# Spreading a pooled row and a bias over the partitions by transfers through device memory in a fused gate-and-attention kernel

## The reference

```
x  = x + gate(gn(x)) * gn(x)                # gn: group norm, 32 groups of 4 channels
x  = x + attention(gn(x))

gate:      pooled[c] = mean over the pixels
           pos[k, c] = clip(c + k - 1 + conv3(pooled)[k, c], 0, 127)      # 3 taps
           out[c]    = sum_k w[k] * (linear interpolation of pooled at pos[k, c]) + b
           gate[c]   = sigmoid(out[c])
attention: value = Wv x + bv;  key, query = two layers of 1x1 conv + batch norm + relu
           27 neighbours (3 x 3 at distances 1, 2 and 4), softmax of query . key over them
           context = sum of weight * value;  out = Wo context + bo
```

## Time and profile before

| | |
|---|---|
| median of 3 runs | 1546.72 us (1544.78 to 1551.17) |
| profiled execution | 1545.68 us, of which span 1543.9 us |
| TensorE busy | 1481.4 us (96%), clock 0.997 of full speed |
| VectorE, ScalarE, GpSimd busy | 1211.6, 1168.4, 776.1 us |
| chain that ended last | TensorE 78%, ScalarE 7%, VectorE 5%, transfers 3% |
| x load, store of 1568 KB, issue to landing | 7.2 us, 5.4 us (medians of 32) |

### The profile page before, as it was taken

The page is one execution under the profiler, slowest core; times in us unless marked ns, Lnnn a source line. Parts: engine busy times, 40 slices in busy tenths (PEclk is TensorE's granted clock), DMA queues, the critical chain, the costliest instruction groups (busy, mean ns, idle before and its releaser), DMA issues.

```text
span 1543.9 us, 35552 instructions
## 1 busy us (share of the span) xinstructions
PE 1481.4 (96%) x9287; PEld 1199.6 (78%) x9287; DVE 1211.6 (78%) x4620; ACT 1168.4 (76%) x3044; POOL 776.1 (50%) x2194
## 2 busy tenths in 40 slices
PE   1899999999999999999999999999999999999998
PEld 1587878888887888878888888888887887878776
DVE  6587878888887887878888888888878887878766
ACT  2577777777777777777777777777777777777776
POOL 5544455555465454455454455545455544455520
PEclk9999999999999999999999999999999999999999
DMA  3135453435453445553445553435454445453324
GB/s 132 47 106 160 151 160 114 136 112 162 149 163 107 137 114 154 156 157 113 136 116 155 156 162 113 139 107 162 149 163 119 135 114 154 148 163 113 96 67 138
DMA packets 104276, 205.98 MB, mean 133 GB/s; under 512 B 13584, under 2 KB 83600, under 8 KB 95888
## 3 DMA queue, kind: packets, MB, share of 16 engines
q1 hardware_dynamic: 104080, 203.72, 44.3%
HBM read 51.62 MB, written 51.38 MB: 67 GB/s over the span
## 4 chain that ended last, share of the span: by engine, by line
PE 78%; ACT 7%; DVE 5%; issue 5%; DMA 3%; SPq 1%; POOL 1%; ACTq 0%; DVEq 0%; POOLq 0%
PE ps_s L416 18%; PE ps_o L449 15%; PE ps_p L471 11%; PE ps_v L489 10%; PE ps_p L466 9%; PE ps_t L428 9%; DMA ksp<-kk 3%; PE ps_o L454 3%; ACT eT L599 2%; ACT e L584 2%; DVE e L946 1%; ACT qq L610 1%; ACT hid L634 1%; DVE e L929 1%; SPq L359 1%
## 5 line engine op out<-in xcount | busy, mean ns | idle before, releaser
L584 ACT ACTIVATE e<-e,zmin 128x256 f32<-128x256 f32 x800 | 404.1, 505 | 209.8 <-DVE zmin L929 201.8
L929 DVE CUSTOM_DVE_ANT_0 e<-ps_s,mask 128x256 f32<-128x256 f32 x800 | 337.3, 422 | 150.2 <-PE ps_s L416 144.1
L449 PEld LDWEIGHTS ps_o<-eT,v 128*128 128x128 f32 x2688 | 377.8, 191 | 74.0 <-issue 69.6
L449 PE MATMUL ps_o<-eT,v 128*128 128x128 f32 x2688 | 433.8, 276 | 0.5 <-ACT eT L599 0.3
L416 PE MATMUL ps_s<-kk,qq 128*128 128x256 f32 x1408 | 428.0, 386 | 0.0
L428 PE MATMUL ps_t<-ident,e 128*128 128x128 f32 x1600 | 306.0, 273 | 0.2 <-DVE e L946 0.2
L428 PEld LDWEIGHTS ps_t<-ident,e 128*128 128x128 f32 x1600 | 225.4, 141 | 81.1 <-DVE e L946 0.5
L599 ACT ACTIVATE eT<-ps_t 128x512 f32<-128x512 f32 (+1 forms) x416 | 235.0, 565 | 63.8 <-PE ps_t L428 61.6
L946 DVE SCALAR_TENSOR_TENSOR e<-e,rz,keep 128x256 f32<-128x256 f32 x480 | 251.6, 524 | 0.0
L416 PEld LDWEIGHTS ps_s<-kk,qq 128*128 128x128 f32 x1408 | 221.4, 192 | 35.7 <-issue 29.5
L471 PE MATMUL ps_p<-hid,w2T 128*128 128x448 f32 x448 | 214.6, 561 | 9.7 <-ACT hid L634 9.7
(11 more groups left out here) (147 smaller groups left out, 1917.8 us busy)
## 6 DMA issues: line engine op xcount, KB each, us to landing
raw<-in_x_dram SPq DMA_DIRECT2D x32, 1568.0 KB, 7.2
out_dram<-raw SPq DMA_DIRECT2D x32, 1568.0 KB, 5.4
v<-v SPq DMA_DIRECT2D x192, 224.0 KB, 3.2
kk<-kk SPq DMA_DIRECT2D x192, 112.0 KB, 2.2
ksp<-kk SPq DMA_DIRECT2D x192, 64.0 KB, 2.5
v<-v_last SPq DMA_DIRECT2D x64, 128.0 KB, 2.9
kk<-kk SPq DMA_DIRECT2D x32, 224.0 KB, 2.9
v<-v_last SPq DMA_DIRECT2D x64, 96.0 KB, 2.7
```

Source lines behind the costliest of these rows:

```text
L449: last = nc.tensor.matmul(o[:, UPIX * (u - 1):UPIX * (u + 1)], v[:, s, u, :], eT[:, UPIX * (base + 2 * u - 1):UPIX * (base + 2 * u + 1)], ...
L584: nc.scalar.activation(e[:, i, :], e[:, i, :], ACT.Exp, bias=zmin[:, i:i + 1], scale=-1.0, accum_out=zs[:, i:i + 1]).then_inc(e_done.next( ...
L929: nc.vector.tensor_tensor_reduce(e[:, i, :], ps_s[(TILES * n.parity() + t) % 2][:, 0:KEYS], mask[:].rearrange("p s h a b -> p (s h a b)"), ...
```

## The change

The row `pooled_row` and the row `bias` no longer come from products. The pooled column `PL` (128 partitions, one float each) is written by a transfer (s1) to a 4 x 128 scratch in device memory, `spread_row`, and read back into all partitions by a second one (s2). `c6` multiplies by the column `Y_B` instead of by `yb_row`, which gives one column; VectorE adds the constant part into the column `VB`, and two more transfers (s3, s4) spread it as `bias`. `diag`, `yb_row`, `bv_row`, the product c3 and VectorE's copy of its result are gone; `wobv` becomes a column. All four transfers are issued by SyncE, at the head of its slot, and each waits for the one before. The slots:

| step | before | after |
|---|---|---|
| LOAD | 15 | 13 |
| s1, s2, s3, s4 | - | 18, 19, 35, 36 |
| c3 | 19 | gone (19 kept for the tables) |
| d4 / a4, p4 | 20 / 21 | 22 / 23 |
| d6, a6 / d7, p7 | 25 / 26 | 26 / 27 |
| c4 / d9, p9 | 27 / 28 | 28 / 29 |
| c6 / d13 | 36 / 37 | 33 / 34 |

```diff
-LOAD = 15
+LOAD = 13
+CH = dict(aggr=12, c1=13, d1=14, c2=15, d3=16, p3=16, s1=18, s2=19, c3=19, d4=22, a4=23, p4=23, d6=26,
+          a6=26, d7=27, p7=27, c4=28, d9=29, p9=29, c5=30, d11=31, p11=31, pw=32, c6=33, d13=34, s3=35, s4=36)
+CHAIN_READS = ((2, "d1"), (4, "d3"), (13, "d9"), (15, "d11"), (17, "d13"))
...
# SyncE, called at the head of its slot
+                    def chain(m, at):
+                        i = m.parity()
+                        if at == CH["s1"]:
+                            sp.wait_ge(pg.sem, pg.count(m, 6))
+                            sp.wait_ge(pooled_in.sem, pooled_in.count(m + -2, 16))
+                            sp.dma_start(spread_row[i, :].unsqueeze(1), col(PL)).then_inc(pooled_out.next(16), 16)
+                        if at == CH["s2"]:
+                            sp.wait_ge(pooled_out.sem, pooled_out.count(m, 16))
+                            sp.wait_ge(dg.sem, dg.count(m + -1, 10))
+                            sp.dma_start(pooled_row[:], spread_row[i, :].partition_broadcast(P)
+                                         ).then_inc(pooled_in.next(16), 16)
+                        if at == CH["s3"]:
+                            sp.wait_ge(dg.sem, dg.count(m, 17))
+                            sp.wait_ge(bias_in.sem, bias_in.count(m + -2, 16))
+                            sp.dma_start(spread_row[2 + i, :].unsqueeze(1), col(VB)).then_inc(bias_out.next(16), 16)
+                        if at == CH["s4"]:
+                            sp.wait_ge(bias_out.sem, bias_out.count(m, 16))
+                            sp.wait_ge(v_done.sem, v_done.count(m + -2, COLUMNS))
+                            sp.dma_start(bias[:, i, :], spread_row[2 + i, :].partition_broadcast(P)
+                                         ).then_inc(bias_in.next(16), 16)
...
# TensorE
-                        if at == CH["c3"]:
-                            pe.wait_ge(pg.sem, pg.count(m, 7))
-                            nc.tensor.matmul(ps_v[:, 8:8 + P], ones[:], diag[:], start=True, stop=True).then_inc(cg.next(), 1)
...
-                            nc.tensor.matmul(ps_v[:, P:2 * P], yb_row[:], wvoT[:], start=True,
+                            nc.tensor.matmul(ps_v[:, 1:2], wvoT[:], col(Y_B + m.parity()), start=True,
...
# GpSimd
-                                  lambda: gp.tensor_scalar(diag[:], ident[:], col(PL), None, ALU.mult))
...
-                                  lambda: gp.tensor_scalar(yb_row[:], ones[:], col(Y_B + i), None, ALU.mult),
...
# VectorE
+                            dve.wait_ge(bias_in.sem, bias_in.count(m, 16))          # values, b == 0
...
-                            dve.wait_ge(cg.sem, cg.count(m, 3))
-                            step(5, nc.vector.tensor_copy(pooled_row[:], ps_v[:, 8:8 + P]))
+                            dve.wait_ge(pooled_in.sem, pooled_in.count(m, 16))      # d4
...
-                            step(18, nc.vector.tensor_tensor(bias[:, m.parity(), :], ps_v[:, P:2 * P], wobv[:],
-                                                             ALU.add))
+                            dve.wait_ge(bias_out.sem, bias_out.count(m + -1, 16))
+                            step(17, nc.vector.tensor_tensor(col(VB), ps_v[:, 1:2], wobv[:], ALU.add))
```

More of the change, by code:

```diff
@@ L394, in _ @@
                         slot(n, t)
-                    for transfers in x_in + stored + k_copied + [v_copied]:
+                    for transfers in x_in + stored + k_copied + [v_copied, pooled_out, pooled_in, bias_out, bias_in]:
                         sp.wait_ge(transfers.sem, transfers.here)
@@ L772, in chain @@
                         if at == CH["p9"]:
-                            gp.wait_ge(dg.sem, dg.count(m, 14))
-                            steps(23,
+                            gp.wait_ge(dg.sem, dg.count(m, 13))
+                            steps(22,
                                   lambda: gp.tensor_tensor(col(BM), col(D1), col(M1), ALU.subtract),
@@ L900, in tables @@
                             nc.vector.tensor_scalar(w2_s[:], w2_s[:], bn_s[:, 1:2], None, ALU.mult).then_inc(v_w, 1)
-                            nc.vector.tensor_scalar(bv_row[:], ones[:], bv_s[:, 0:1], None, ALU.mult).then_inc(v_w, 1)
+                            dve.wait_ge(v_w, 2)
                         if t == CH["d3"] + 1:
@@ L1002, in chain @@
                                                                accum_out=col(POS + k)).then_inc(dg.next(), 1)
-                            dve.wait_ge(dg.sem, dg.count(m, 8))
-                            step(9, nc.vector.tensor_tensor(col(POS, 3), col(POS, 3), base_f[:], ALU.add))
-                            step(10, nc.vector.tensor_scalar(col(POS, 3), col(POS, 3), 0.0, P - 1.0, ALU.max, ALU.min))
+                            dve.wait_ge(dg.sem, dg.count(m, 7))
+                            step(8, nc.vector.tensor_tensor(col(POS, 3), col(POS, 3), base_f[:], ALU.add))
+                            step(9, nc.vector.tensor_scalar(col(POS, 3), col(POS, 3), 0.0, P - 1.0, ALU.max, ALU.min))
                         if at == CH["d6"]:
-                            dve.wait_ge(pg.sem, pg.count(m, 15))
-                            step(11, nc.vector.scalar_tensor_tensor(junk[:], pooled_row[:], 1.0, hat_sum[:],
+                            dve.wait_ge(pg.sem, pg.count(m, 14))
+                            step(10, nc.vector.scalar_tensor_tensor(junk[:], pooled_row[:], 1.0, hat_sum[:],
                                                                    ALU.mult, ALU.mult, accum_out=col(ZS)))
@@ L1011, in chain @@
                             dve.wait_ge(ag.sem, ag.count(m, 4))
-                            step(12, nc.vector.tensor_scalar(col(EX), col(EX), 1.0, None, ALU.add))
-                            step(13, nc.vector.reciprocal(col(GATE), col(EX)))
+                            step(11, nc.vector.tensor_scalar(col(EX), col(EX), 1.0, None, ALU.add))
+                            step(12, nc.vector.reciprocal(col(GATE), col(EX)))
                         if at == CH["d9"]:
-                            dve.wait_ge(cg.sem, cg.count(m, 4))
@@ L1019, in chain @@
+                            step(14, nc.vector.scalar_tensor_tensor(col(SQ1), col(D1), col(D1), col(AV),
                                                                     ALU.mult, ALU.add))
                         if at == CH["d11"]:
+                            dve.wait_ge(cg.sem, cg.count(m, 4))
+                            step(15, nc.vector.tensor_scalar(col(VE1), ps_v[:, 3:4], EPS, None, ALU.add))
+                        if at == CH["d13"]:
                             dve.wait_ge(cg.sem, cg.count(m, 5))
-                            step(16, nc.vector.tensor_scalar(col(VE1), ps_v[:, 3:4], EPS, None, ALU.add))
```

76 lines of the change are left out of this document (38 added, 38 removed).

## The result

The changed kernel takes 2034.66 us (median of 4 runs, 2027.51 to 2036.74) against 1547.33 us before (median of 4 runs too): 1.314 times as long, 95% interval 1.310 to 1.318. The forecast was 1723 us. The sign and both places of loss were right, the size was not: 487 us were lost where 176 were forecast.

What follows compares the result with a forecast made beforehand. TensorE was taken as the bound, busy 1481.4 of 1543.9 us. 1545.7 - 6.6 (products) + 105 (gate) + 70 (load) + 8 (start) = 1722, as median 1723 us; own range 1677 to 1785, wider range 1610 to 1790.

Steps and rivals of the forecast that it cites:

- both places of loss: TensorE waiting for M1 before c4, +3.5 us an image, and for keys 6 in slot 17, 2.4 us.
- TensorE's products: Slot 19 loses the spread of `diag`, 0.22 us an image, 6.6 us less; narrowing c6's second product wins 0.
- The gate's slots: Later hats make VectorE wait 1.7 us at d6 and delay c4: +3.5 us an image, 105 us (75 to 135).
- The load in front of the keys: With LOAD = 13 keys 6 land behind the load; TensorE waits 2.4 us in slot 17, 29 images, 70 us.
- the 1.9 us of the forecast without s4's delay: Slot 17's wait for keys if small writes take 1.6 us and s4 costs SyncE nothing; 29 x 1.9 = 55 us.
- The four small transfers: s1 to s4 at 2.5 us each; pooled row hidden, s4 holding SyncE 0.5 us before value copies, load, keys 6.
- keep 1.6 and 4.7: Bounds for a small transfer: a 5 KB load at 1.6 us, the 0.5 KB load of `bv_s` at 4.7 us.
- the upper bounds of all parts: Gate's slots 135 us, slot 17's wait for keys 133 us (29 x 4.6), start 14 us.
- The start: Before the first scores nothing hides image 0's chain: +4.5 us, image 1's gate 3.5; together +8 us (2 to 14).
- Rival 4: Small writes slow: s3 at 4.7 us or more makes SyncE the second bound; 1785 us or more, chance 0.09.

Runs made afterwards that it cites:

- b2_load13: The kernel before with LOAD = 13 instead of 15 alone, so the load stands in front of keys 6; 1689.28 us (1.089).
- x6_grouped: The changed kernel with only the scratch laid out in groups of 8 words, 512 bytes from group to group; 1877.56 us (1.212).
- x5_apart: The changed kernel with the words of s1 and s3 written 2 KB apart, s2 and s4 reading a row of x instead; 1851.01 us (1.194).
- b4_d6: The kernel before, products kept, with c3 21, d4 22, a4 and p4 23, d6 and a6 28, later gate steps moved along; 1601.88 us (1.034).
- v1_pooled: The kernel before with the pooled row by transfers in groups of 8 words, bias still by product, LOAD = 15, later gate slots; 1528.98 us (0.987).
- x7_all: The changed kernel with scratch in groups of 8 words, LOAD = 15 and later slots, both rows by transfers; 1543.95 us (0.998).

## Why the prediction was wrong, point by point

**TensorE's products: right.** Slot 19 is 1.63 us instead of 1.85, the 0.22 us of the sum. The narrowed product of c6 wins nothing, as the prediction had it from the earlier trace rows: in the kernel after, slots 8, 9 and 11 together are as long as before (2.22 + 1.93 + 2.07 = 6.22 us, before 1.85 + 1.87 + 2.52 = 6.24), although c6 moved from one to the other.

**The gate's slots: place, chain and waits right, size short by the clock.** GpSimd's p4 and VectorE's d6 after, on their timelines:

```profile
1005.81 0.30 POOL L773 TENSOR_SCALAR hats<-hats 128x128 f32<-128x128 f32 x1 [25.39 <-ACT hats L667]
...
1010.15 0.45 POOL L777 TENSOR_TENSOR hat_sum<-hat_sum,hats 128x128 f32<-128x128 f32 x1
...
1013.95 0.27 POOL L790 TENSOR_TENSOR g<-g,st 128x1 f32<-128x1 f32 x1
```

```profile
1010.64 0.29 DVE L1029 SCALAR_TENSOR_TENSOR junk<-pooled_row,hat_sum 128x128 f32<-128x128 f32 x1 [1.68 <-POOL hat_sum L777]
```

p4 runs from 1005.81 to 1010.60, 4.8 us as in the earlier trace rows. VectorE waited 1.68 us for it (forecast 1.7), and c4 2.49 us for M1 (forecast 761.9 to 764.2, 2.3). Slots 0 to 3 are 3.2 us longer than before (forecast 3.3). Slot 4 at the start of the image (950.55 to 955.03) is 1.7 us longer, where the forecast had 0.2. In all +5.0 us against +3.5.

**The load in front of the keys: right in kind.** b2_load13 has no s4, so its wait is to be set beside the 1.9 us of the forecast without s4's delay: slot 16 is 2.9 us longer in the image shown and 3.1 in the median one. The keys landed 9.1 us after the load's issue, where 8.2 were forecast. "Lands behind it" is not to be taken to the letter: there the kk copy, issued 0.7 us after the load, took 7.4 us and landed at 956.94, 0.2 us before the load, and the second ksp copy 0.8 us after it. What the sum lacked besides is the 1.7 us of slots 17 and 18 behind it.

**The four small transfers: the step that failed.** "I take 2.5 us ..., and keep 1.6 and 4.7." It took 6.9 us, outside both bounds. The nearest row by name, `bv_s` at 4.7 us, was a read of device memory; the page had no write of neighbouring words, and the bounds came from transfers of another kind. Even the upper bounds of all parts taken together (135, 133 and 14) give 1821 us. The prediction had named the right victims: "Behind s4 stand the value copies (728.91 today), the load and keys 6." In the image shown, ksp came 7.7 us later than forecast (a wait of 10.2 us instead of 2.4), set off against slot 16 of the kernel before. s4 is issued 4.8 us later, as s3 took 7.2 us from issue to issue and not 2.5. From s4 to the load it is 6.6 us and not 4.5, since the issue of the first value copy lasts 2.7 us where it took 0.46 before; this happens in 13 of the 32 images, and why is open. From the load's issue to ksp it is 9.0 us and not 8.2. The new layout of the scratch takes 157 us off (x6_grouped), the distance of 2 KB with reads of x 184 (x5_apart).

The fixed cost of about 2.0 us that the Trainium skill (DMA: Bandwidth & Descriptors, Anatomy of one DMA) gives, weighed in the prediction, is near what the spaced writes take here, 1.7 to 2.0 us at 2 KB, and what the grouped ones take in three of five cases, 1.8 us. For neighbouring words it is off by a factor of 3.5: the measured 6.9 us decides.

**Not in the sum at all: the clock after a wait.** The prediction added waits and took all products at their old length. In the image shown, slots 17, 18 and 4 are 2.0, 0.4 and 1.7 us longer for the same products, at clocks of 0.50 to 0.9. That is 4.1 us of 18.1. For the whole run the busy line gives it: TensorE is busy 1586.1 us, before 1481.4, although 6.6 us of products are gone, so the remaining products took about 111 us longer, of the 487; I put this to the lower clock, which no run held fixed. The mean granted clock of the run is 0.906.

The account of one image, from the slots: ksp 10.2 (forecast 2.4), slots 17 and 18 2.4 (0), slots 0 to 4 5.0 (3.5), slot 13, where keys 5 are late behind the same s3, 0.7 (0), product -0.2 (-0.2): 18.1 us against 5.7. The mean image loses 15.5, and 30 of them 464 us. **The start** costs 16.9 us (first scores at 71.78 instead of 54.89) against 8, and this too is mostly the slow write: in x6_grouped the first scores stand at 57.94.

**The rivals.** Rival 4 named the mechanism that came (s3 holds SyncE) and gave it a chance of 0.09, but priced it with the same upper bound, 1785 us. With 6.9 us in its sum the wait of slot 17 would be 6.8 us instead of 4.6, 29 x 6.8 = 197 us instead of 133, and the time 1849: still 186 us short, of which 111 are products that took longer. Its place was right, its price was bounded by a row of another kind.

## What to carry to other kernels

An unknown price is bounded only by rows of the same kind: same direction, same memory, same layout of the pieces. Where no such row exists, the range has to stay open upward if a queue waits for the transfer. Where a change makes TensorE wait, the work behind the wait is to be priced at the lower clock too: here 2.9 us of wait in b2_load13 cost 1.7 us more, and 10.2 us in the changed kernel 2.4. The 1.5 us of slot 0 in b4_d6 cost nothing more, so both cases belong in the range. And when steps of a chain are moved, write down for each pair the time between them on the timeline and the slots between them; a4 to d6 had 1.65 us to spare in 4 slots and lost one.

## What was not expected of the hardware

A write of 128 words from 128 partitions into 512 neighbouring bytes of device memory took 6.2 to 7.3 us; the same words 64 bytes apart took 1.8 to 1.9, and 16 groups of 8 words 1.8 to 3.4. A scratch of 16 rows with 8 words each makes the spread of a column take 2.1 + 2.9 us (medians of x6_grouped) instead of 6.9 + 4.0. Behind a load the same grouped write took 3.4 us (v1_pooled) and 4.7 (x7_all).

TensorE's granted clock went from 1.00 to 0.50 during a wait of 10 us (0.78 in the mean of that window), stayed there for the 3.9 us of slot 17 and was 0.90 in the next 4 us. In the same image a wait of 1.0 us in slot 0 left it at 1.00; behind that and the 2.5 us before c4 it was 0.63 on average in slot 4.
